# The last attention of a four-layer gated block on Trainium2: context tile of the weighting one unit later, rows of reciprocals by transposes, head 0's maximum in two parts

## The chip, the cores and the metric

The kernel runs on one core of one Trainium2 chip. It computes a chain of four gated cross-attention and feed-forward layers in one launch. The metric is the device time of one execution in microseconds, and the time of a kernel is the median over its runs. Engines are named as the profile names them: PE (matmuls and transposes; PEld is its weight load), DVE (vector work), ACT (activations and copies), POOL (copies), SP (it issues DMAs).

## The reference, cut to what matters

Eight sub-layers follow each other. The change is in the seventh, the last attention. Its queries come from the tokens of two batches (1024 tokens of 256 numbers each), its keys and values from the 1024 normalised token rows and the 77 normalised context rows of the same batch, with 16 heads of 64:

```python
def _L3_xattn_ref(x, latents, mask, g_x, b_x, g_l, b_l, Wq, Wkv, Wout, g_o, b_o):
    xn = layer_norm(x, g_x, b_x)
    ln = layer_norm(latents, g_l, b_l)
    q = jnp.einsum('bnd,de->bne', ln, Wq)
    kv_in = jnp.concatenate([xn, ln], axis=1)
    k, v = jnp.split(jnp.einsum('bnd,de->bne', kv_in, Wkv), 2, axis=-1)
    q, k, v = (split_heads(q), split_heads(k), split_heads(v))
    sim = jnp.einsum('bhid,bhjd->bhij', q * scale, k)
    attn = jax.nn.softmax(jnp.where(full_mask[:, None, None, :], sim, max_neg), axis=-1)
    out = jnp.einsum('bhij,bhjd->bhid', attn, v)
    return layer_norm(jnp.einsum('bne,ed->bnd', out.transpose(0, 2, 1, 3).reshape(b, m, INNER), Wout), g_o, b_o)

x = x + jnp.tanh(g_xattn[3]) * _L3_xattn_ref(ctx_1024, _layernorm(x), mask, ...)
```

In the call the block's tokens take the place of `latents` and the 77 context rows that of `x`. So each query has 1101 scores: 77 under the mask (context) and 1024 of tokens. All of it is fp32.

## The kernel before, in words

The stage works in 128 units. A unit is 128 queries of two neighbouring heads (h = 0 and 1) of one batch; eight units (u % 8 is the block of queries) make one pair of heads n = u // 8, and two units make one group g = u // 2. Each engine has its own program over the loop index u, and they meet by semaphores. PE works through this at each index u:

- `scores(u)`: four score blocks of 128 x 512 tokens and two of 128 x 77 context columns, into PSUM banks 0 to 4. Head 0 has words 0 to 1100 and head 1 words 1459 to 2559. They may start once both exponentials of unit u-1 have read their scores (semaphore `a6_p`).
- `ctx_turn(u-1)`: two transposes (L1214, L1215) of the context columns of the weights of unit u-1.
- At even u, `sums_turn`: the reciprocals of the sums of the group g = (u-2)/2 are spread over 64 partitions and turned into rows, by four matmuls with the identity matrix.
- At even u below 120, two of the eight pieces of the next pair's queries, keys and values (u % 8 = 0, 2, 4, 6 takes pieces 0 and 1, 2 and 3, 4 and 5, 6 and 7).
- At odd u, `weigh((u-3)/2)`: nine tiles of keys (eight of tokens, one of the context), two heads each, into one bank. This is 18 matmuls, and 36 in the trace, since an fp32 matmul stands there as two.
- At even u for the last four groups of each batch (`(u//2-2) % 32 >= 28`, so u = 60 to 66 and 124 to 130), `project`: the output projection, 16 matmuls of 256 columns, 32 in the trace.
- At eight odd u (N7), a transpose of rows for the next stage.

An fp32 matmul of a whole array is long: 256 columns take about 0.21 us for each of the two that the trace shows.

DVE: at even u it first multiplies the weighted values of a group by its rows of reciprocals (L2516). Then for every unit it adds the mask to the context scores (L2519), takes the maximum of head 1's context (L2520), that of head 0's 1101 scores (L2522), that of head 1's 1024 tokens (L2523), joins the two of head 1 (L2524), transposes the weights in 32 x 32 blocks once they are there (L2532, twice), and at odd u takes four reciprocals (L2537). ACT: copies the context transposes out of PSUM (L1781), at even u the rows of reciprocals (L1785), then takes the two exponentials with their sums (L1796), and at even u copies the two pieces (L1748 to L1756). POOL and SP's DMAs move the transposed blocks of the weights into place for `weigh` (16 blocks of a unit, half of them each).

The transposes, rows, pieces and products that leave PE share three PSUM banks (5, 6, 7) in turn: each takes the bank of the one three before it, once that one has been copied. The order is written out by hand in all five programs, and every engine works strictly in its own order.

## Time and profile before

| | |
|---|---|
| median of 3 runs | 2086.64 us (2085.38 to 2089.72) |
| the profiled execution | 2084.4 us |
| its span | 2082.6 us |
| PE busy | 1921.5 us, 92% |
| DVE busy | 1435.7 us, 69% |
| ACT busy | 978.5 us, 47% |
| POOL busy | 752.3 us, 36% |
| the stage of the change | from about 1105 us to about 1989 us of the span |

The profile shows one execution. The 128 units of the last attention take most of 885 us. A timeline row gives start, length, engine, line, operation, what is written and read, and how many instructions were merged into it; a bracket gives the idle time before it and what ended it. The sum of lengths of PE is more than the time, since a matmul's end is modelled and the next starts before it. A unit's length is best read from one first context transpose (L1214) to the next.

### The profile page before, as it was taken

The numbers are of one execution on the slowest core, as the hardware profiler recorded it, in microseconds if no ns is written. First come the engines' busy times: TensorE is split into PE (matmuls) and PEld (weight loads), VectorE is DVE, ScalarE is ACT, GpSimd is POOL, SyncE is SP. The second block draws the span as 40 slices with busy tenths as digits, with TensorE's granted clock in tenths as the row PEclk, the third lists the DMA queues.
The fourth block names the chain that finished last, engine by engine and source line by source line (L and its number), as shares of the span: only waits on it lengthen the run. The fifth ranks groups of instructions, "written<-read, shape, count | busy, mean of one in ns | idle before, by whom it ended". The sixth has DMA issues, their size and how long they took to land.

```text
span 2082.6 us, 33216 instructions
## 1 busy us (share of the span) xinstructions
PE 1921.5 (92%) x11797; PEld 1355.2 (65%) x11797; DVE 1435.7 (69%) x2676; ACT 978.5 (47%) x2079; POOL 752.3 (36%) x1145
## 2 busy tenths in 40 slices
PE   6997799696999988997878999999999999998999
PEld 3885799542699976883565666666675666655644
DVE  5775111467344457787867999999878999998755
ACT  5672333343111252226875555555545555555455
POOL 1002111000522200000006777777656777777500
PEclk9897899898999999998989999999999999999999
DMA  3702899502489960002002333333222333333201
GB/s 115 208 2 79 273 323 333 170 1 86 163 292 321 310 228 1 1 1 86 1 13 60 82 83 82 83 83 83 72 57 72 82 82 82 82 82 81 63 1 41
DMA packets 191184, 226.87 MB, mean 109 GB/s; under 512 B 28939, under 2 KB 167085, under 8 KB 191021
## 3 DMA queue, kind: packets, MB, share of 16 engines
q1 hardware_dynamic: 183725, 201.98, 33.0%
q0 software_dynamic: 7296, 22.78, 3.3%
q8 instruction: 95, 1.56, 0.3%
q14 instruction: 68, 0.56, 0.1%
HBM read 127.64 MB, written 29.91 MB: 76 GB/s over the span
## 4 chain that ended last, share of the span: by engine, by line
PE 45%; ACT 6%; DVE 3%; issue 1%; POOL 0%; ACTq 0%; DVEq 0%; POOLq 0%
PE ps L640 41%; ACT w_odd L1796 4%; PE ps L1214 2%; PE ps L1215 1%; ACT arena L1785 1%; PE ps L1106 0%; DVE w_odd L2532 0%; DVE small L2410 0%; POOL arena L1908 0%; ACT out_feat L1708 0%; PE ps L1115 0%; ACT xn_tok L1651 0%; DVE small L2522 0%; ACT out_feat L1714 0%; DVE arena L2380 0%
## 5 line engine op out<-in xcount | busy, mean ns | idle before, releaser
L1908 POOL COPY arena<-w_odd 32x512 f32<-32x512 f32 x1024 | 623.7, 609 | 254.4 <-DVE w_odd L2532 202.1
L640 PE MATMUL ps<-arena,w_odd 128*128 128x128 f32 (+4 forms) x2352 | 468.2, 441 | 3.0 <-DVE arena L2202 1.2
L640 PE MATMUL ps<-arena 128*64 128x256 f32 (+4 forms) x3248 | 392.3, 370 | 8.3 <-DVE arena L2333 4.4
L640 PEld LDWEIGHTS ps<-arena 128*64 128x64 f32 (+4 forms) x3248 | 258.9, 155 | 119.5 <-issue 22.6
L2532 DVE STREAM_TRANSPOSE w_odd<-w_odd 128x1024 f32<-128x1024 f32 x256 | 317.4, 1245 | 14.6 <-ACT w_odd L1796 3.0
L1796 ACT ACTIVATE w_odd<-ps,small 128x1101 f32<-128x1101 f32 x256 | 301.6, 1179 | 48.0 <-DVE small L2522 41.0
L640 PEld LDWEIGHTS ps<-arena,w_odd 128*128 128x128 f32 (+3 forms) x2352 | 286.3, 188 | 27.9 <-issue 18.7
L1781 ACT ACTIVATE arena<-ps 77x256 f32<-77x256 f32 x128 | 48.5, 379 | 295.4 <-PE ps L1215 295.4
L2522 DVE TENSOR_REDUCE small<-ps 128x1 f32<-128x1101 f32 x128 | 166.9, 1304 | 29.3 <-PE ps L640 28.1
L1893 POOL DMA_INDIRECT token_rows<-arena x62 | 59.8, 964 | 292.3 <-DVE arena L2223 292.3
L2523 DVE TENSOR_REDUCE small<-ps 128x1 f32<-128x1024 f32 x128 | 155.4, 1214 | 0.0
L640 PE MATMUL ps<-xn_feat,w_even 128*128 128x512 f32 (+1 forms) x352 | 139.5, 528 | 5.1 <-DVE xn_feat L2446 2.1
L1889 POOL DMA_INDIRECT expert_rows_in<-xn_tok,arena x48 | 46.4, 966 | 266.3 <-DVE arena L2186 252.3
L640 PEld LDWEIGHTS ps<-w_even,w_odd 64*128 64x128 f32 x512 | 86.5, 188 | 85.3 <-ACT w_odd L1796 65.9
L1903 POOL TENSOR_TENSOR x_res<-x_res,w_even 128x4096 f32<-128x4096 f32 x1 | 8.8, 8843 | 350.6 <-ACT xn_tok L1767 350.6
L640 PE MATMUL ps<-w_even,w_odd 64*128 64x77 f32 x512 | 100.8, 277 | 20.5 <-ACT w_odd L1796 19.9
L1580 ACT ACTIVATE arena<-ps,arena 128x128 f32<-128x128 f32 x184 | 67.3, 367 | 93.1 <-PE ps L640 82.3
L640 PE MATMUL ps<-arena,w_even 128*128 128x256 f32 (+2 forms) x608 | 107.6, 330 | 0.5 <-DVE x_res L1983 0.5
L640 PE MATMUL ps<-xn_feat,w_odd 128*128 128x512 f32 x224 | 103.5, 603 | 0.0
L640 PE MATMUL ps<-w_even,xn_feat 128*128 128x128 f32 (+1 forms) x576 | 100.9, 322 | 1.3 <-DVE xn_tok L2516 1.3
L640 PE MATMUL ps<-w_odd,arena 128*128 128x256 f32 (+1 forms) x436 | 101.5, 380 | 0.0
L640 PEld LDWEIGHTS ps<-arena,w_even 128*128 128x128 f32 x608 | 94.7, 192 | 8.4 <-DVE x_res L1983 0.6
(398 smaller groups left out, 2909.8 us busy)
## 6 DMA issues: line engine op xcount, KB each, us to landing
arena<-w_odd SPq DMA_DIRECT2D x1024, 64.0 KB
w_odd<-in_s_w SPq DMA_DIRECT2D x32, 1024.0 KB, 7.4
w_odd<-in_s_wgu SPq DMA_DIRECT2D x30, 704.0 KB, 6.1
w_even<-in_s_w SPq DMA_DIRECT2D x15, 1024.0 KB, 7.3
arena<-expert_rows_in SPq DMA_DIRECT2D x62, 130.0 KB, 4.7
w_odd<-in_s_wd SPq DMA_DIRECT2D x30, 256.0 KB, 3.6
out_feat<-in_s_wgu SPq DMA_DIRECT2D x10, 704.0 KB, 5.9
expert_rows_in<-zero_row POOLq DMA_DIRECT2D x1, 5070.0 KB, 33.2
```

What stands on the lines that cost most here:

```text
L640: return pe.matmul(o, lhsT, rhs, start=start, stop=stop, **kw)
L1214: pe.transpose(PS[0:C, bank, 0:P], s6_p[u % 2][0][:, S:KV], ident[:, :])
L1215: pe.transpose(PS[0:C, bank, P:2 * P], s6_p[u % 2][1][:, 0:C], ident[:, :]).then_inc(r6_mm, 1)
L1580: act.activation(s1_h[q][:, m], PS[:, (M * i + m) % 4, 0:TS], ACT.Gelu, bias=s1_bt[w][:, m:m + 1]).then_inc(per["mu_act", 1], 1)
L1781: act.activation(s6_ptc[g % 2][:, :, c0:c0 + P], PS[0:C, bank, 0:2 * P].rearrange("p (h n) -> p h n", h=2), ACT.Copy).then_inc(r6_act, 1)
L1796: act.activation(s6_p[u % 2][h], s6_sc[h], ACT.Exp, bias=s6_nm[:, u % 2, h:h + 1], accum_out=s6_sm[:, g % 2, 2 * (u % 2) + h:2 * (u % 2) + ...
L1889: pool.indirect_dma_start(xs_dram[st], bass.IndirectOffsetOnAxis(ap=pos_i[:, j, t:t + 1], axis=0), XNE[:, t, :], None)\
L1893: pool.indirect_dma_start(yt_dram[st], bass.IndirectOffsetOnAxis(ap=es_t[:, i:i + 1], axis=0), mx_y[st][i % 2][:, 0], None)\
L1908: pool.tensor_copy(s6_d[u % 4][32 * j:32 * j + 32, :, 256 * i:256 * i + 256], s6_pm[u % 2][32 * i:32 * i + 32, :, 256 * j:256 * j + 256]). ...
L2522: dve.tensor_reduce(s6_nm[:, u % 2, 0:1], s6_sc[0], AX.X, ALU.max, negate=True).then_inc(a6_mx, 1)
L2523: link(dve.tensor_reduce(s6_cm[:, u % 2, 1:2], psf[:, 3 * 512:3 * 512 + S], AX.X, ALU.max, negate=True))
L2532: dve.transpose(s6_pm[u % 2][:, h], s6_pm[u % 2][:, h]).then_inc(t6_done, 1)
```

## The change

Three things are changed in the last attention.

The context tile of `weigh` leaves the odd index. `weigh_tokens(g)` does the eight token tiles at u = 2g+3, and `weigh_context(g)` the ninth at u = 2g+4, behind `sums_turn`. Its products have bank 5 for themselves, while everything else alternates between banks 6 and 7. The multiplication by the reciprocals on DVE moves from the head of the even unit to its end, and the projection comes two indices later (`u//2-3` for `u//2-2`), so it stands at u = 62 to 68 and 126 to 132.

The rows of reciprocals are made by transposes. ACT copies the four reciprocals of a group into a 128 x 256 tile (`s6_rb`, each of them 64 times; L1800 of the change), with a new semaphore `r6_bc`; PE waits for it and transposes the two halves (L1227 of the change) in place of four matmuls.

Head 0's maximum is taken in two parts: words 0 to 511 (bank 0), which are full when the mask may be added, and words 512 to 1100 after the last scores. A third reduction of the two results gives the negated maximum.

PE, an odd unit and the even one behind it (u % 8 = 6), before. L640 is the helper of all matmuls; `ps<-arena 64x256` are the products of weights and values, `ps<-ident,small` the rows of reciprocals, `w_odd` holds queries and weights, `xn_feat` the normalised tokens.

```order
L640 MATMUL ps<-arena 64x256 x18
L640 MATMUL ps<-w_even,w_odd 128x77
L640 MATMUL ps<-arena,w_odd 128x512 x2
L640 MATMUL ps<-w_even,w_odd 128x77
L640 MATMUL ps<-arena,w_odd 128x512 x2
L1214 MATMUL ps<-ident,w_odd 77x128
L1215 MATMUL ps<-ident,w_odd 77x128
L640 MATMUL ps<-ident,small 64x128 x4
L640 MATMUL ps<-w_even,xn_feat 128x128 x8
L640 MATMUL ps<-xn_feat,w_even 128x256 x2
```

The same place in the change (L643 is the helper now, L1219 and L1220 the context transposes):

```order
L643 MATMUL ps<-arena 64x256 x16
L643 MATMUL ps<-w_even,w_odd 128x77
L643 MATMUL ps<-arena,w_odd 128x512 x2
L643 MATMUL ps<-w_even,w_odd 128x77
L643 MATMUL ps<-arena,w_odd 128x512 x2
L1219 MATMUL ps<-ident,w_odd 77x128
L1220 MATMUL ps<-ident,w_odd 77x128
L1227 MATMUL ps<-ident,arena 128x128 x2
L643 MATMUL ps<-arena 64x256 x2
L643 MATMUL ps<-w_even,xn_feat 128x128 x8
L643 MATMUL ps<-xn_feat,w_even 128x256 x2
```

Two of the 18 products have moved behind the rows of reciprocals of the even unit; and these are two transposes of `arena` (the new tile) where four matmuls of `small` stood.

ACT, an even unit (u % 8 = 2), before: context transposes, rows of reciprocals, two exponentials, three copies of pieces.

```order
L1781 ACTIVATE arena<-ps 77x2x128
L1785 ACTIVATE arena<-ps 128x256
L1796 ACTIVATE w_odd,small<-ps,small 128x1101 x2
L1752 ACTIVATE arena<-ps 128x256
L1756 ACTIVATE w_even<-ps 128x77
L1748 ACTIVATE w_odd<-ps 128x512
```

And in the change, where L1800 is the new copy of the reciprocals:

```order
L1794 ACTIVATE arena<-ps 77x2x128
L1800 ACTIVATE arena<-small 128x256
L1804 ACTIVATE arena<-ps 128x256
L1815 ACTIVATE w_odd,small<-ps,small 128x1101 x2
L1765 ACTIVATE arena<-ps 128x256
L1769 ACTIVATE w_even<-ps 128x77
L1761 ACTIVATE w_odd<-ps 128x512
```

The new copy stands between the copy of the context transposes (L1794) and that of the rows (L1804), ahead of the exponentials.

DVE, the end of an odd unit and the even unit behind it, before:

```order
L2532 STREAM_TRANSPOSE w_odd<-w_odd 128x1024 x2
L2537 RECIPROCAL small<-small 128x4
L2516 TENSOR_TENSOR out_feat<-ps,arena 128x256
L2519 TENSOR_TENSOR ps<-ps,w_even 128x2x77
L2520 TENSOR_REDUCE small<-ps 128x1
L2522 TENSOR_REDUCE small<-ps 128x1
L2523 TENSOR_REDUCE small<-ps 128x1
L2524 TENSOR_REDUCE small<-small 128x1
```

And in the change:

```order
L2546 STREAM_TRANSPOSE w_odd<-w_odd 128x1024 x2
L2551 RECIPROCAL small<-small 128x4
L2531 TENSOR_TENSOR ps<-ps,w_even 128x2x77
L2532 TENSOR_REDUCE small<-ps 128x1
L2533 TENSOR_REDUCE small<-ps 128x1
L2535 TENSOR_REDUCE small<-ps 128x1
L2536 TENSOR_REDUCE small<-small 128x1
L2537 TENSOR_REDUCE small<-ps 128x1
L2538 TENSOR_REDUCE small<-small 128x1
L2546 STREAM_TRANSPOSE w_odd<-w_odd 128x1024 x2
L2558 TENSOR_TENSOR out_feat<-ps,arena 128x256
```

The multiplication (L2516, now L2558) has gone from ahead of the mask (L2519, now L2531) to behind the two block transposes of the even unit; head 0's maximum is L2533, L2535 and L2536 in place of L2522.

```diff
@@ -220,6 +220,7 @@
         s6_k = [cut(AR, 9216 + 1024 * i, S) for i in range(2)]
         s6_v = [cut(AR, 11264 + 1152 * i, NKT, P) for i in range(2)]
         s6_r = [cut(AR, 13568 + 256 * i, 2 * P) for i in range(2)]
+        s6_rb = [cut(AR, 14080 + 256 * i, 4, DH) for i in range(2)]
         s6_z = [cut(AR, 14592 + 512 * i, 2, D) for i in range(2)]
         s6_cnt = cut(AR, 15616, KD, B * C)
         s6_mb = small[:, 568:568 + 40].bitcast(U8)[:, 0:B * C].rearrange("p (b c) -> p b c", b=B)
...
@@ -383,12 +385,12 @@
             batch = [("c", u - 1)] if turn else []
             if even and 2 <= u < NU + 2:
                 batch += [("r", (u - 2) // 2)]
+            if even and 4 <= u < NU + 4:
+                batch += [("v", (u - 4) // 2)]
             if even and u // 8 < 15:
                 batch += [("w", u // 8 + 1, u % 8), ("w", u // 8 + 1, u % 8 + 1)]
-            if not even and 3 <= u < NU + 3:
-                batch += [("v", (u - 3) // 2)]
-            if even and u >= 4 and (u // 2 - 2) % 32 >= 28:
-                batch += [("o", u // 2 - 2)]
+            if even and u >= 6 and (u // 2 - 3) % 32 >= 28:
+                batch += [("o", u // 2 - 3)]
             if u in N7:
                 batch += [("n", N7[u])]
             for key in batch:
...
@@ -396,13 +398,14 @@
                 done[eng] += 1
                 r6_no[key] = len(r6_no)
                 r6_sb[key] = (r6_act if eng == "act" else r6_dve, done[eng])
-        r6_keys = list(r6_no)
+        r6_keys = [key for key in r6_no if key[0] != "v"]
+        r6_turn = {key: i for i, key in enumerate(r6_keys)}
 
         PIECES = (("q", 0, 512), ("k", 768, S), ("v", 0, 2), ("q", 512, S), ("v", 6, NKT), ("k", 0, 512), ("v", 2, 6), ("k", 512, 768))
 
         def r6_bank(key):
 
-            return 5 + r6_no[key] % 3
+            return 5 if key[0] == "v" else 6 + r6_turn[key] % 2
 
         def copied(eng, key):
 
...
@@ -1175,9 +1178,11 @@
 
                 def free_bank(key):
 
-                    t = r6_no[key]
-                    if t >= 3:
-                        copied(pe, r6_keys[t - 3])
+                    if key[0] == "v":
+                        if key[1]:
+                            copied(pe, ("v", key[1] - 1))
+                    elif r6_turn[key] >= 2:
+                        copied(pe, r6_keys[r6_turn[key] - 2])
                     return r6_bank(key)
 
                 def scores(u):
...
@@ -1216,32 +1221,38 @@
 
                 def sums_turn(g):
 
-                    pe.wait_ge(a6_rb, g + 1)
+                    pe.wait_ge(r6_bc, g + 1)
                     bank = free_bank(("r", g))
                     for i in range(2):
-                        for h in range(2):
-                            r = 64 * h
-                            last = mm(PS[r:r + 64, bank, i * P:(i + 1) * P], s6_rc[:, g % 2, 2 * i + h:2 * i + h + 1].broadcast_to([P, DH]), ident[:, :])
+                        last = pe.transpose(PS[:, bank, i * P:(i + 1) * P], s6_rb[g % 2][:, 2 * i:2 * i + 2].rearrange("p a b -> p (a b)"), ident[:, :])
                     last.then_inc(r6_mm, 1)
 
-                def weigh(g):
+                def weigh_tile(g, i, bank):
 
                     n = g // 4
+                    s0 = 2 * g % 4
+                    rows = P if i < NKT - 1 else C
+                    for h in range(2):
+                        r = 64 * h
+                        if i < NKT - 1:
+                            p = s6_dw[:, s0:s0 + 2, h].rearrange("p u (q i n) -> p u q i n", q=4, i=8)[:, :, :, i]
+                        else:
+                            p = s6_ptc[g % 2][:, h]
+                        last = mm(PS[r:r + 64, bank, 0:2 * P], s6_v[n % 2][0:rows, i, r:r + 64], p, start=(i == 0), stop=(i == NKT - 1))
+                    return last
+
+                def weigh_tokens(g):
+
                     moved(pe, 2 * g)
                     moved(pe, 2 * g + 1)
+                    bank = free_bank(("v", g))
+                    for i in range(NKT - 1):
+                        weigh_tile(g, i, bank)
+
+                def weigh_context(g):
+
                     copied(pe, ("c", 2 * g + 1))
-                    bank = free_bank(("v", g))
-                    s0 = 2 * g % 4
-                    for i in range(NKT):
-                        rows = P if i < NKT - 1 else C
-                        for h in range(2):
-                            r = 64 * h
-                            if i < NKT - 1:
-                                p = s6_dw[:, s0:s0 + 2, h].rearrange("p u (q i n) -> p u q i n", q=4, i=8)[:, :, :, i]
-                            else:
-                                p = s6_ptc[g % 2][:, h]
-                            last = mm(PS[r:r + 64, bank, 0:2 * P], s6_v[n % 2][0:rows, i, r:r + 64], p, start=(i == 0), stop=(i == NKT - 1))
-                    last.then_inc(r6_mm, 1)
+                    weigh_tile(g, NKT - 1, r6_bank(("v", g))).then_inc(r6_mm, 1)
 
                 def project(g):
 
...
@@ -1273,13 +1284,15 @@
                         ctx_turn(u - 1)
                     if even and 2 <= u < NU + 2:
                         sums_turn((u - 2) // 2)
+                    if even and 4 <= u < NU + 4:
+                        weigh_context((u - 4) // 2)
                     if even and n < 16:
                         for i in (j, j + 1):
                             piece(n, i, free_bank(("w", n, i))).then_inc(r6_mm, 1)
                     if not even and 3 <= u < NU + 3:
-                        weigh((u - 3) // 2)
-                    if even and u >= 4 and (u // 2 - 2) % 32 >= 28:
-                        project(u // 2 - 2)
+                        weigh_tokens((u - 3) // 2)
+                    if even and u >= 6 and (u // 2 - 3) % 32 >= 28:
+                        project(u // 2 - 3)
                     if u in N7:
                         t = N7[u]
                         pe.wait_ge(ln_xn, NT * xn_no[ln_no[7]] + t + 1)
...
@@ -1781,6 +1794,12 @@
                         act.activation(s6_ptc[g % 2][:, :, c0:c0 + P], PS[0:C, bank, 0:2 * P].rearrange("p (h n) -> p h n", h=2), ACT.Copy).then_inc(r6_act, 1)
                     if even and 2 <= u < NU + 2:
                         g = (u - 2) // 2
+                        act.wait_ge(a6_rb, g + 1)
+                        if g >= 2:
+                            act.wait_ge(r6_mm, r6_no["r", g - 2] + 1)
+                        act.activation(s6_rb[g % 2], s6_rc[:, g % 2].unsqueeze(2).broadcast_to([P, 4, DH]), ACT.Copy).then_inc(r6_bc, 1)
+                    if even and 2 <= u < NU + 2:
+                        g = (u - 2) // 2
                         bank = filled(("r", g))
                         act.activation(s6_r[g % 2], PS[:, bank, 0:2 * P], ACT.Copy).then_inc(r6_act, 1)
                     if u < NU:
...
@@ -2507,19 +2526,14 @@
                     piece(0, j, j).then_inc(c6_sb, 1)
                 for u in range(NU + 6):
                     even = u % 2 == 0
-                    if even and 4 <= u < NU + 4:
-                        g = (u - 4) // 2
-                        c = (g // 4) % 8
-                        q0 = 2 * P * (g % 4)
-                        bank = filled(("v", g))
-                        copied(dve, ("r", g))
-                        dve.tensor_tensor(s6_ot[c][:, q0:q0 + 2 * P], PS[:, bank, 0:2 * P], s6_r[g % 2], ALU.mult).then_inc(r6_dve, 1)
                     if u < NU:
                         dve.wait_ge(a6_s, 4 * u + 3)
                         link(dve.tensor_tensor(s6_both, s6_both, s6_mk[:, u // 64].unsqueeze(1).broadcast_to([P, 2, C]), ALU.add))
                         dve.tensor_reduce(s6_cm[:, u % 2, 0:1], s6_both[:, 1], AX.X, ALU.max, negate=True)
+                        dve.tensor_reduce(s6_hm[:, u % 2, 0:1], psf[:, 0:512], AX.X, ALU.max, negate=True)
                         dve.wait_ge(a6_s, 4 * u + 4)
-                        dve.tensor_reduce(s6_nm[:, u % 2, 0:1], s6_sc[0], AX.X, ALU.max, negate=True).then_inc(a6_mx, 1)
+                        link(dve.tensor_reduce(s6_hm[:, u % 2, 1:2], psf[:, 512:KV], AX.X, ALU.max, negate=True))
+                        dve.tensor_reduce(s6_nm[:, u % 2, 0:1], s6_hm[:, u % 2], AX.X, ALU.min).then_inc(a6_mx, 1)
                         link(dve.tensor_reduce(s6_cm[:, u % 2, 1:2], psf[:, 3 * 512:3 * 512 + S], AX.X, ALU.max, negate=True))
                         dve.tensor_reduce(s6_nm[:, u % 2, 1:2], s6_cm[:, u % 2], AX.X, ALU.min).then_inc(a6_mx, 1)
                     if u == 0:
...
@@ -2533,14 +2547,21 @@
                         if not even:
                             g = u // 2
                             if g >= 2:
-                                dve.wait_ge(r6_mm, r6_no["r", g - 2] + 1)
+                                dve.wait_ge(r6_bc, g - 1)
                             dve.reciprocal(s6_rc[:, g % 2], s6_sm[:, g % 2]).then_inc(a6_rb, 1)
-                    if even and u >= 6 and 28 <= (u // 2 - 3) % 32 < 31:
-                        added(u // 2 - 3)
-                    if even and u >= 4 and (u // 2 - 2) % 32 >= 28:
-                        normed(u // 2 - 2)
-                    if not even and u >= 5 and ((u - 1) // 2 - 2) % 32 == 31:
-                        added((u - 1) // 2 - 2)
+                    if even and 4 <= u < NU + 4:
+                        g = (u - 4) // 2
+                        c = (g // 4) % 8
+                        q0 = 2 * P * (g % 4)
+                        bank = filled(("v", g))
+                        copied(dve, ("r", g))
+                        dve.tensor_tensor(s6_ot[c][:, q0:q0 + 2 * P], PS[:, bank, 0:2 * P], s6_r[g % 2], ALU.mult).then_inc(r6_dve, 1)
+                    if even and u >= 8 and 28 <= (u // 2 - 4) % 32 < 31:
+                        added(u // 2 - 4)
+                    if even and u >= 6 and (u // 2 - 3) % 32 >= 28:
+                        normed(u // 2 - 3)
+                    if not even and u >= 7 and ((u - 1) // 2 - 3) % 32 == 31:
+                        added((u - 1) // 2 - 3)
                     if u == 72:
                         row_vars7(0)
                     if u == 74:
```

## Rows read from the trace of the kernel before

**Rows 1.** Busy time by engine, one window (us, instructions); then clock, DMA share, GB/s
```profile
1200.00:1300.00 100.00, 98.97 (x680) 61.93 (x678) 90.88 (x125) 55.48 (x107) 75.43 (x125) 1.00 0.35 84
```

**Rows 2.** Timeline (start, length), PE: first context transpose, units 20 to 25
```profile
1230.68 0.33 PE L1214 MATMUL ps<-ident,w_odd 128*77 128x128 f32 x1
...
1237.02 0.34 PE L1214 MATMUL ps<-ident,w_odd 128*77 128x128 f32 x1
...
1243.58 0.34 PE L1214 MATMUL ps<-ident,w_odd 128*77 128x128 f32 x1
...
1249.82 0.33 PE L1214 MATMUL ps<-ident,w_odd 128*77 128x128 f32 x1
...
1256.37 0.33 PE L1214 MATMUL ps<-ident,w_odd 128*77 128x128 f32 x1
...
1262.61 0.34 PE L1214 MATMUL ps<-ident,w_odd 128*77 128x128 f32 x1
```

**Rows 3.** Timeline of units 24 and 25, all engines
```profile
1254.23 0.69 PE L640 MATMUL ps<-arena,w_odd 64*128 64x512 f32 x1
...
1255.06 0.13 DVE L2537 RECIPROCAL small<-small 128x4 f32<-128x4 f32 x1
...
1255.65 0.33 DVE L2519 TENSOR_TENSOR ps<-ps,w_even 128x154 f32<-128x154 f32 x1
...
1256.01 0.24 DVE L2520 TENSOR_REDUCE small<-ps 128x1 f32<-128x77 f32 x1
...
1256.48 1.30 DVE L2522 TENSOR_REDUCE small<-ps 128x1 f32<-128x1101 f32 x1 [0.23 <-PE ps L640]
...
1256.74 0.66 PE L640 MATMUL ps<-ident,small 128*64 128x128 f32 x8
...
1256.85 0.38 ACT L1781 ACTIVATE arena<-ps 77x256 f32<-77x256 f32 x1 [2.99 <-PE ps L1215]
...
1257.33 2.85 PE L640 MATMUL ps<-xn_feat,w_even 128*128 128x512 f32 x8
...
1257.44 0.38 ACT L1785 ACTIVATE arena<-ps 128x256 f32<-128x256 f32 x1 [0.22 <-PE ps L640]
...
1257.90 1.18 ACT L1796 ACTIVATE w_odd<-ps,small 128x1101 f32<-128x1101 f32 x1
...
1258.98 0.19 ACT L1796 ACTIVATION_READ_ACCUMULATOR w_odd<-ps,small 128x1 f32 x1
...
1260.47 0.33 PE L640 MATMUL ps<-w_even,w_odd 64*128 64x77 f32 x1 [0.29 <-ACT w_odd L1796]
...
1262.98 4.11 PE L640 MATMUL ps<-arena 128*64 128x256 f32 x36
...
1267.02 0.33 PE L640 MATMUL ps<-w_even,w_odd 64*128 64x77 f32 x1
```

**Rows 4.** Timeline, PE, unit 62: fourth pair of pieces, then the projection
```profile
1508.55 2.05 PE L640 MATMUL ps<-w_even,xn_feat 128*128 128x128 f32 x16
...
1511.30 1.89 PE L640 MATMUL ps<-w_even,xn_tok 128*128 128x256 f32 x8
```

**Rows 5.** Groups by line and shape: an ACT copy from SBUF, two DVE maxima
```profile
L1640 ACT ACTIVATE arena<-arena 128x256 f32<-128x256 f32 x16 | 6.4, 401 | 0.0
...
L2522 DVE TENSOR_REDUCE small<-ps 128x1 f32<-128x1101 f32 x128 | 166.9, 1304 | 29.3 <-PE ps L640 28.1
...
L2520 DVE TENSOR_REDUCE small<-ps 128x1 f32<-128x77 f32 x128 | 30.4, 237 | 4.4
```

**Rows 6.** Timeline, PE, the last projections (units 128 to 130)
```profile
1970.42 2.00 PE L640 MATMUL ps<-w_even,xn_tok 128*128 128x256 f32 x8
...
1977.53 4.11 PE L640 MATMUL ps<-arena 128*64 128x256 f32 x36
...
1982.16 2.00 PE L640 MATMUL ps<-w_even,xn_tok 128*128 128x256 f32 x8 [0.53 <-DVE out_feat L2516]
```

**Rows 7.** Busy time by engine in a window without pieces (units 122 and 123)
```profile
1923.00:1930.00 7.00, 3.93 (x21) 2.45 (x20) 5.34 (x7) 3.27 (x6) 4.74 (x9) 0.79 0.30 72
```

7 lines of the change are left out of this document (4 added, 3 removed).

## The prediction

> **What bounds the kernel now.** I read the busy time by window first: in the middle of the stage PE is at 98.97 of 100 us, DVE at 90.88, ACT at 55.48, with a granted clock of 1.00 [rows 1]. That alone says nothing of what ends last, so I took one cycle of units from the first context transposes of the timeline [rows 2]. Odd units last 6.55 us (from 1249.82 to 1256.37). Even units last 6.34 us at u = 20 and 6.24 us at u = 22 and 24; u % 8 = 2 goes like u = 20. So there are two limits.
>
> The timeline of u = 24 shows the first one [rows 3]. Call S the start of its scores, 1254.23. The scores are ready at S+2.25, where DVE begins head 0's maximum (1256.48); this takes 1.30; the first exponential starts at S+3.67 (1257.90); two exponentials, 2.57 us, lead to the next scores at 1260.47, S+6.24. This chain of scores, maximum, two exponentials and scores is the limit of even units at u % 8 = 0 and 6. The second limit is PE's own work. In the odd unit the products start at 1262.98 and the next scores at 1267.02: 4.04 us for 36 matmuls, 0.112 each, and they end 0.31 us after the chain would have allowed. At u % 8 = 2 and 4 the pieces are longer and PE is over by 0.10.
>
> In the even unit PE reaches the rows of reciprocals at 1256.74 (S+2.51), and the pieces at 1257.33 (S+3.10) [rows 3].
>
> **The change, odd units.** Four matmuls of the trace go: 4 x 0.112 = 0.45. PE would be at 6.10, so the chain is the limit. Its part that changes is the maximum. Two rows give its cost: 77 elements take 0.237 and 1101 take 1.304 [rows 5], so 1.042 ns an element and a fixed 0.157. The mask is added at S+1.42 and head 1's context maximum starts at S+1.78 [rows 3]. Head 0's first part can follow about 0.16 later, at S+1.94, and the second at S+2.54 (a start-to-start of about 0.60, with 0.08 of overlap); by then all scores are there. It takes 0.157 + 589 x 0.001042 = 0.77 and ends at S+3.31; the small joining reduction is another 0.16 with 0.03 before it, S+3.50. Before it was S+3.55 (1256.48 + 1.30). So the split gives 0.05, not the half maximum that one might expect: its first part hides under the scores, but the second has its own fixed cost and so has the third. I take 6.20 for an odd unit, 0.35 less. Bounds: 0.25 less (the parts cost 0.1 more than I think) and 0.40 less. There are 60 such units (u = 3 to 125 without two that are longer for other reasons), so -21.0 us, with -15 and -24 as bounds.
>
> The Trainium skill speaks against the split: "VectorE: DVE Perf Modes", section on the errata of operands in SBUF, says that an operation pays its fixed latency once for a large tile and again for each small one. Its figures, 120 cycles at 0.96 GHz for a PSUM source and 58 for SBUF, give an estimate of 0.19 us for the two added reductions. The rows give 0.16 for each, 0.24 with the overlap of 0.08 taken off. By the page an odd unit would come out 0.05 shorter, 3 us in the sum; the measured durations stand.
>
> **The change, even units.** Here is the new wait. PE may not transpose the reciprocals until ACT has spread them, and ACT does that behind the copy of the context transposes, which PE has made just before. The reciprocals themselves are there early (1255.06, S+0.83) [rows 3] and ACT is idle for 2.99 us before the copy (bracket of 1256.85) [rows 3], but the new copy stands behind that one in ACT's order. So: context copy at S+2.62; 0.38 long with 0.10 of overlap with what follows (1257.90 + 1.18 against 1258.98) [rows 3], so the spreading starts at S+2.90; an ACT copy of 128 x 256 from SBUF takes 0.40 [rows 5]; PE goes on at S+3.35, with 0.05 for the semaphore (as 0.04 to 0.05 from a last exponential to the scores). PE idles 0.84 us where it idled none. Two transposes cost 0.30 (the two context transposes took 0.37, 1256.37 to 1256.74 [rows 2, 3], and matmul rows of 128 columns as short as 0.11 each), in place of 0.59. Then the context tile, 4 x 0.112 = 0.45. The pieces start at S+4.10 for S+3.10: 1.00 later. Queued behind the wait on PE are the context tile, both pieces and the next scores. Bounds: 0.76 later (spreading 0.35, transposes 0.22, context 0.43) and 1.15 later (no overlap on ACT, transposes 0.37).
>
> ACT's exponentials are late too. The rows leave PE about 0.48 after the first transpose starts (1256.37 to 1256.85, the same for the context) [rows 2, 3], S+3.83; the copy of the rows holds ACT for 0.28; the first exponential starts at S+4.11 in place of S+3.67. The chain is 6.24 + 0.43 = 6.67, with +0.28 and +0.59 as bounds. The maximum is ready long before, so the split gives nothing here.
>
> Which of both limits counts depends on the pieces:
> - u % 8 = 0: pieces 2.57 (2.85 busy, less some 0.28 by which the last modelled end passes the next start) [rows 3]. PE 6.67, chain 6.67: +0.43. 13 units without a projection: +5.6.
> - u % 8 = 2 and 4: PE was the limit, so all of it counts: 28 units x 1.00 = +28.0.
> - u % 8 = 6: pieces 2.75 (1508.55 to 1511.30) [rows 4]; 4.10 + 2.75 = 6.85 for 6.24: 14 x 0.61 = +8.5.
> - 4 units with pieces and projection, PE bound: 4 x 1.00 = +4.0.
> - u = 120, 122, 124 without pieces +0.43 each, 126 with a projection +1.00: +2.3.
>
> Sum +48.4; with the bounds +35 and +57. The other edits here cost nothing: the multiplication on DVE ends at about S+8.2 (two block transposes of 2.5 us in all from S+5.4, then 0.3), when the mask of the next unit is due at S+6.67+1.42 = S+8.09 or later, so 0.1 at most at u % 8 = 0; PE's banks are free in time, as each one's copy is over a unit before.
>
> **The end of the stage.** A projection takes 7.1 us (1970.42 to 1977.53) [rows 6]. At u = 124 none is left, so that unit falls from 10.0 (3.10 + 6.9) to 6.67, -3.4. At the end there is one more than before: u = 128 holds an earlier group's, and behind the last weighting (from 1977.53, 4.04 long) stand two instead of one: +7.0. The wait before the last (1977.53 + 4.04 to 1982.16, some 0.6, of which DVE's multiplication) goes: -0.6; the spreading behind the reciprocals at u = 128 adds 0.3 there. Net +3.3. The first batch's projections move into like units, +0.
>
> Sum: 48.4 - 21.0 + 3.3 = +30.7 us. Against the profiled execution's 2084.4 that is 2115.1. The median of the runs is 2086.64, 2.2 above that execution, so 2117 for the median. With all bounds on one side: 35 - 24 + 3 = +14 (2101) and 57 - 15 + 4 = +46 (2133).
>
> **The rivals.**
> 1. The spreading is hidden. If ACT had spread the reciprocals before S+2.5, PE would not wait: pieces at S+2.51+0.30+0.45 = S+3.26, only 0.16 later. Then u % 8 = 2 and 4 and projections cost 32 x 0.16 = 5.1, the rest nothing, odd units -21.0, the end +3.3: -12.6, 2074. For it: the reciprocals are ready at S+0.83 and ACT idles. Against it: ACT's order in the change. It decides the sign: the change is faster if the spreading ends before about S+2.9 instead of S+3.3. Chance 0.06.
> 2. The stall is partly covered and the gain and the loss cancel, 2083 to 2091: it needs a shift of the pieces of about 0.4, outside my bounds. Chance 0.05.
> 3. The split makes the chain longer. If the maximum begins only when the last scores are there (a first part that waits, or a late DVE), the three take 0.60 + 0.77 + 0.03 + 0.16 = 1.56 in place of 1.30, and the chain of the 60 odd units is 6.50 instead of 6.20: +18, so 2135. For it DVE is at 91% [rows 1]; against it is the idle of 0.23 before head 0's maximum in the same unit [rows 3]. Chance 0.12.
> 4. PE's clock. In a stretch where PE was busy 3.93 of 7.00 us the granted clock was 0.79 [rows 7], so in part the lower level of 1.2 GHz; in the middle of the stage it was 1.00 [rows 1]. The change puts 0.84 us of idle into every even unit. If a tenth of the units had their scores (2.2 us long) at 1.2 GHz, 2.2 us each more, that is 13 x 2.2 = +29: 2146. Against it: with 0.84 idle in 13.2 us PE is still busy over 90%, while rows 7 have 56%. Chance 0.08. The Trainium skill, "TensorE: Matmul & The Clock Gate", part on the transpose in PE mode, says that transposes do not count as busy for the clock; two more of them would then make this rival likelier, but the context transposes stand in every unit of rows 1 at a clock of 1.00, so I give it no more.
>
> **How the numbers follow.** My forecast has 0.69, rivals 1 to 4 have 0.06, 0.05, 0.12 and 0.08. A change of under 0.2% (4 us) can't be told from none. Faster is rival 1 and a bit of 2: 0.07; within 0.2%: 0.05; slower the rest: 0.88. Range 2100 to 2136: the forecast's bounds and rival 3, leaving out rivals 1, 2 and 4.
>
> **What would show it.** In the profile after: the copy by ACT of `arena` from `small` starts about 0.28 after the context copy, and PE's transposes of `arena` have some 0.8 us of idle before them, released by ACT; odd units are 6.2 and even ones 6.7, 7.3, 7.3 and 6.85 long; the second part of head 0's maximum ends about 3.3 after the scores' start. It is wrong if PE has no idle before those transposes, if odd units stay at 6.5, or if the clock of the middle falls below 1.00.

## The result, and the profile after

The changed kernel takes 2139.07 us (median of 4 runs, 2135.69 to 2140.45); the kernel before took 2086.01 beside it (4 runs). The ratio is 1.0249 [1.0231, 1.0267]. The direction was forecast; the forecast of 2117 is 22 us too low, and the time lies above the range. The profiled execution took 2140.45 us with a span of 2138.7, 56.1 more than before.

The busy time of the same window as [rows 1], after:

```profile
1200.00:1300.00 100.00, 94.00 (x594) 56.51 (x596) 87.24 (x147) 54.57 (x111) 71.91 (x119) 1.00 0.33 79
```

PE has lost 5 us of 100 to idle, at an unchanged clock of 1.00. The first context transposes, which answer to [rows 2], for u = 19 to 23:

```profile
1233.46 0.33 PE L1219 MATMUL ps<-ident,w_odd 128*77 128x128 f32 x1
1239.63 0.33 PE L1219 MATMUL ps<-ident,w_odd 128*77 128x128 f32 x1
1247.18 0.33 PE L1219 MATMUL ps<-ident,w_odd 128*77 128x128 f32 x1
1253.34 0.33 PE L1219 MATMUL ps<-ident,w_odd 128*77 128x128 f32 x1
1260.50 0.33 PE L1219 MATMUL ps<-ident,w_odd 128*77 128x128 f32 x1
```

Odd units last 6.17 and 6.16 (6.55 before), the even one at u = 20 (u % 8 = 4) lasts 7.55 (6.34) and that at u = 22 (u % 8 = 6) 7.16 (6.24). The timeline of unit 22, all engines, answers to [rows 3]; its scores start at S = 1251.20:

```profile
1251.20 0.33 PE L643 MATMUL ps<-w_even,w_odd 64*128 64x77 f32 x1
...
1252.35 0.14 DVE L2551 RECIPROCAL small<-small 128x4 f32<-128x4 f32 x1
1252.63 0.33 DVE L2531 TENSOR_TENSOR ps<-ps,w_even 128x154 f32<-128x154 f32 x1
...
1253.14 0.68 DVE L2533 TENSOR_REDUCE small<-ps 128x1 f32<-128x512 f32 x1
...
1253.74 0.76 DVE L2535 TENSOR_REDUCE small<-ps 128x1 f32<-128x589 f32 x1
1253.82 0.38 ACT L1794 ACTIVATE arena<-ps 77x256 f32<-77x256 f32 x1 [2.67 <-PE ps L1220]
1254.10 0.40 ACT L1800 ACTIVATE arena<-small 128x256 f32<-128x256 f32 x1
1254.54 0.15 DVE L2536 TENSOR_REDUCE small<-small 128x1 f32<-128x2 f32 x1
1254.56 0.44 PE L1227 MATMUL ps<-ident,arena 128*128 128x128 f32 x2 [0.77 <-ACT arena L1800]
...
1254.93 0.65 PE L643 MATMUL ps<-arena 77*64 77x256 f32 x4
1255.03 0.38 ACT L1804 ACTIVATE arena<-ps 128x256 f32<-128x256 f32 x1 [0.53 <-PE ps L1227]
1255.32 1.18 ACT L1815 ACTIVATE w_odd<-ps,small 128x1101 f32<-128x1101 f32 x1
1255.51 2.05 PE L643 MATMUL ps<-w_even,xn_feat 128*128 128x128 f32 x16
...
1258.36 0.33 PE L643 MATMUL ps<-w_even,w_odd 64*128 64x77 f32 x1
```

PE has finished both context transposes and stands for 0.77 us until ACT has spread the reciprocals (L1800), which it does at once behind the context copy (L1794). The reciprocals had been there since 1252.49, and ACT idle for 2.67 before the copy. From the first context transpose to the transposes of the spread tile it is 1.22, where the old rows followed after 0.37: 0.85 more. The same wait stands in every even unit. All instructions of L1227 on PE:

```profile
L1227 PE MATMUL ps<-ident,arena x128: 272/327/475, 1119.7 to 2016.3; 128*128 128x128 f32 x128
its engine sat idle before it (us, times) until:
  ACT arena L1800: 50.1, 64
```

50.1 us in 64 waits. In step with it the exponential starts at S+4.12 (forecast S+4.11), and the pieces at S+4.31 where they stood at S+3.10. The split of the maximum ends at S+3.49 (1254.54 + 0.15; forecast S+3.50).

Where the 56.1 us of span went, by the first context transposes (c0 is that of index 1, c119 that of index 120; the last line goes from c125, at index 126, to the end of the program):

| stretch | before | after | difference | forecast |
|---|---|---|---|---|
| ahead of c0 | 1107.07 | 1110.62 | +3.55 | 0 |
| c0 to c119 | 801.13 | 842.83 | +41.7 | +26.1 |
| c119 to c125 | 45.61 | 44.32 | -1.3 | -3.1 |
| behind c125 | 128.8 | 140.9 | +12.1 | +7.7 |

The first line is not the change's: the instructions there are the same, and four experiments below that leave them as they are too have c0 at 1107.29, 1107.46, 1109.67 and 1110.15. The granted clock of 600 to 800 was 0.95 in this execution and 0.98 before. The last line is the end of the stage, PE, which answers to [rows 6]:

```profile
2016.01 0.69 PE L1227 MATMUL ps<-ident,arena 128*128 128x128 f32 x2 [1.34 <-ACT arena L1800]
2016.62 1.12 PE L643 MATMUL ps<-arena 77*64 77x256 f32 x4
2017.68 3.78 PE L643 MATMUL ps<-w_even,xn_tok 128*128 128x256 f32 x8
2021.25 2.67 PE L643 MATMUL ps<-w_even,out_feat 128*128 128x256 f32 x8
2023.76 1.89 PE L643 MATMUL ps<-w_even,xn_tok 128*128 128x256 f32 x8
...
2027.30 4.11 PE L643 MATMUL ps<-arena 128*64 128x256 f32 x36
2031.34 1.99 PE L643 MATMUL ps<-w_even,xn_tok 128*128 128x256 f32 x8
```

and the busy time and clock of two windows there:

```profile
2010.00:2020.00 10.00, 7.67 (x44) 4.55 (x41) 7.47 (x14) 6.55 (x11) 4.14 (x7) 0.80 0.12 28
2020.00:2030.00 10.00, 10.00 (x54) 7.78 (x54) 2.79 (x11) 0.45 (x2) 0.88 (x2) 0.86 0.11 26
```

Two projections do stand behind the last weighting, as forecast. What was not forecast: PE was idle for 0.99 and 1.34 us a little earlier, and from 2016 to 2022 the granted clock is 0.50, the lower level of 1.2 GHz. The first half of the projection takes 6.08 (2017.68 to 2023.76), the second 3.54 (to 2027.30).

### The profile page after: what moved, and what is told of

The parts are those of the page before. It is cut to its first block, busy times and chain, and to the rows that moved or that the text cites. A ratio compares the mean times of both kernels' runs of the same rounds, so it can differ in the third digit from the quotient of the medians.

```text
span 2138.7 us, 32768 instructions
## 1 busy us (share of the span) xinstructions
PE 1933.3 (90%) x11413; PEld 1341.3 (63%) x11413; DVE 1447.9 (68%) x2932; ACT 994.8 (47%) x2143; POOL 752.6 (35%) x1145
## 4 chain that ended last, share of the span: by engine, by line
PE 46%; ACT 5%; DVE 3%; issue 2%; POOL 0%; ACTq 0%; DVEq 0%
PE ps L643 41%; ACT w_odd L1815 2%; PE ps L1219 1%; PE ps L1227 1%; ACT arena L1800 1%; PE ps L1220 1%; PE ps L1109 1%; DVE w_odd L2546 0%; DVE small L2429 0%; ACT L1826 0%; PE ps L1118 0%; ACT xn_tok L1664 0%; ACT out_feat L1721 0%; DVE small L2535 0%; DVE arena L2502 0%
## 5 line engine op out<-in xcount | busy, mean ns | idle before, releaser
L643 PE MATMUL ps<-arena,w_odd 128*128 128x128 f32 (+4 forms) x2352 | 470.6, 443 | 3.0 <-DVE arena L2221 1.2
L643 PE MATMUL ps<-arena 128*64 128x256 f32 (+4 forms) x3248 | 406.8, 373 | 8.2 <-DVE arena L2352 4.4
L2546 DVE STREAM_TRANSPOSE w_odd<-w_odd 128x1024 f32<-128x1024 f32 x256 | 312.9, 1243 | 46.4 <-ACT w_odd L1815 40.1
L643 PEld LDWEIGHTS ps<-arena 128*64 128x64 f32 (+4 forms) x3248 | 252.9, 155 | 121.9 <-issue 33.8
L643 PEld LDWEIGHTS ps<-arena,w_odd 128*128 128x128 f32 (+3 forms) x2352 | 287.0, 189 | 27.6 <-issue 18.8
L1794 ACT ACTIVATE arena<-ps 77x256 f32<-77x256 f32 x128 | 48.6, 379 | 294.5 <-PE ps L1220 294.5
L643 PE MATMUL ps<-xn_feat,w_even 128*128 128x512 f32 (+1 forms) x352 | 139.5, 528 | 4.9 <-DVE xn_feat L2465 2.1
L643 PEld LDWEIGHTS ps<-w_even,w_odd 64*128 64x128 f32 x512 | 86.9, 189 | 85.1 <-issue 42.3
L643 PE MATMUL ps<-w_even,w_odd 64*128 64x77 f32 x512 | 101.0, 278 | 18.3 <-ACT w_odd L1815 17.0
L643 PE MATMUL ps<-arena,w_even 128*128 128x256 f32 (+2 forms) x608 | 107.8, 330 | 0.5 <-DVE x_res L2002 0.5
L643 PE MATMUL ps<-xn_feat,w_odd 128*128 128x512 f32 x224 | 103.7, 604 | 0.0
L643 PE MATMUL ps<-w_odd,arena 128*128 128x256 f32 (+1 forms) x436 | 101.5, 379 | 0.0
L643 PE MATMUL ps<-w_even,xn_feat 128*128 128x128 f32 (+1 forms) x576 | 100.8, 321 | 0.0
L643 PEld LDWEIGHTS ps<-arena,w_even 128*128 128x128 f32 x608 | 94.8, 192 | 8.6 <-DVE x_res L2002 0.6
L2535 DVE TENSOR_REDUCE small<-ps 128x1 f32<-128x589 f32 x128 | 97.2, 759 | 1.5 <-PE ps L643 1.5
```

Of the source, the lines that this page charges most:

```text
L643: return pe.matmul(o, lhsT, rhs, start=start, stop=stop, **kw)
L1794: act.activation(s6_ptc[g % 2][:, :, c0:c0 + P], PS[0:C, bank, 0:2 * P].rearrange("p (h n) -> p h n", h=2), ACT.Copy).then_inc(r6_act, 1)
L2535: link(dve.tensor_reduce(s6_hm[:, u % 2, 1:2], psf[:, 512:KV], AX.X, ALU.max, negate=True))
L2546: dve.transpose(s6_pm[u % 2][:, h], s6_pm[u % 2][:, h]).then_inc(t6_done, 1)
```

## The experiments

Ratios are to the kernel before, run beside each kernel. The experiments ran on more than one chip (before took 2087.03 beside the first four told here, 2099.88 and 2098.68 beside the others), so ratios are compared, not times.

**The spreading ahead of the context copy.** The changed kernel with one block of ACT moved.

```diff
+act.wait_ge(a6_rb, g + 1)
...
+act.activation(s6_rb[g % 2], s6_rc[:, g % 2].unsqueeze(2).broadcast_to([P, 4, DH]), ACT.Copy).then_inc(r6_bc, 1)
...
 bank = filled(("c", v))
...
-act.wait_ge(a6_rb, g + 1)
...
-act.activation(s6_rb[g % 2], s6_rc[:, g % 2].unsqueeze(2).broadcast_to([P, 4, DH]), ACT.Copy).then_inc(r6_bc, 1)
```

> The changed kernel with one edit: ACT spreads the reciprocals ahead of the copy of the context transposes instead of behind it. Theory 1 (the new wait of PE for ACT is what costs): the 0.77 us of idle before the transposes of the rows goes in all 64 even units; even units fall from 7.55 to 6.70 (u % 8 = 2, 4), from 7.09 to 6.25 (0) and from 7.16 to 6.33 (6); odd ones stay at 6.16 to 6.25; in all about 51 us less, 2088. Rival (the copies on ACT are the limit whatever their order, so the rows and the exponentials stay late): even units stay over 6.9 and the time over 2115.

Measured: 2083.3 us (8 runs), ratio 0.9977 [0.9966, 0.9988]. The timeline of an even unit (u % 8 = 6), ACT and PE:

```profile
1242.36 0.41 ACT L1795 ACTIVATE arena<-small 128x256 f32<-128x256 f32 x1 [1.37 <-DVE small L2551]
1243.18 0.33 PE L1219 MATMUL ps<-ident,w_odd 128*77 128x128 f32 x1
...
1243.46 0.38 PE L1227 MATMUL ps<-ident,arena 128*128 128x128 f32 x2
1243.66 0.38 ACT L1800 ACTIVATE arena<-ps 77x256 f32<-77x256 f32 x1 [0.89 <-PE ps L1220]
1243.78 0.65 PE L643 MATMUL ps<-arena 77*64 77x256 f32 x4
...
1244.36 2.05 PE L643 MATMUL ps<-w_even,xn_feat 128*128 128x128 f32 x16
1244.65 1.18 ACT L1815 ACTIVATE w_odd<-ps,small 128x1101 f32<-128x1101 f32 x1 [0.33 <-DVE small L2536]
```

The bracket of ACT's copy shows it: ACT waits for the reciprocal and for nothing else, and is done at 1242.77, 0.69 us before PE starts its transposes of the spread tile (1243.46). In 63 of 64 even units no idle of PE stands before those transposes, and the exponential waits for the maximum again. Even units are 6.57 or 6.56 (u % 8 = 2, 4), 6.17 (6) and 6.14 (0) long, most odd ones away from the projections 6.16 to 6.28. So the wait made the change slow: 1.0249 to 0.9977 is some 56 us (3.3 of them are a lower clock at the end of the stage, told further down). The two context transposes took 0.28 here (1243.18 to 1243.46), where I had kept 0.37 in the expectation; that is most of why the even units came out 0.11 to 0.16 shorter than expected, and the time 5 us. What is left of the change is faster than before, by 4.8 us (2.5 to 7.1 by the interval) and not by the 12.6 of rival 1; the runs below say why.

**The split alone** (in the kernel before).

```diff
+dve.tensor_reduce(s6_hm[:, u % 2, 0:1], psf[:, 0:512], AX.X, ALU.max, negate=True)
 dve.wait_ge(a6_s, 4 * u + 4)
-dve.tensor_reduce(s6_nm[:, u % 2, 0:1], s6_sc[0], AX.X, ALU.max, negate=True).then_inc(a6_mx, 1)
+link(dve.tensor_reduce(s6_hm[:, u % 2, 1:2], psf[:, 512:KV], AX.X, ALU.max, negate=True))
+dve.tensor_reduce(s6_nm[:, u % 2, 0:1], s6_hm[:, u % 2], AX.X, ALU.min).then_inc(a6_mx, 1)
```

> The kernel before with head 0's maximum in two parts and nothing else. Theory 1 (the first part hides under the scores, the fixed costs eat the rest): the units at the limit of the chain (u % 8 = 0 and 6) fall from 6.24 to 6.19, the others stay; 2084 to 2087. Rival (the two extra reductions lengthen the chain): even units 6.4 to 6.5 and the time 2092 to 2100.

Measured: 2086.64 (10 runs), 0.9998 [0.9988, 1.0008]. The units that the chain bounds (u % 8 = 0, 6) fall from 6.24 to 6.16 or 6.17; the other even units and most odd ones stay at PE's bound. The four odd units behind a projection of the first batch (u = 61 to 67) grow by 0.23 to 0.26, to 6.78, 6.94, 6.85 and 6.85: about 1 us, which takes back half of what the 27 others gave. Nothing in the sum, and rival 3 shows in those four units alone.

**The context tile alone**, with its bank and the later projections, rows by matmuls and one maximum (of the changed kernel).

```diff
-pe.wait_ge(r6_bc, g + 1)
+pe.wait_ge(a6_rb, g + 1)
...
-        last = pe.transpose(PS[:, bank, i * P:(i + 1) * P], s6_rb[g % 2][:, 2 * i:2 * i + 2].rearrange("p a b -> p (a b)"), ident[:, :])
+            last = mm(PS[r:r + 64, bank, i * P:(i + 1) * P], s6_rc[:, g % 2, 2 * i + h:2 * i + h + 1].broadcast_to([P, DH]), ident[:, :])
```

> The changed kernel with the rows of reciprocals by four matmuls as before (no spreading on ACT) and head 0's maximum in one piece; only the context tile, bank 5, the multiplication and the projection are moved. Theory 1 (a change between matmuls of half the array's columns and of the whole array costs PE about 0.1, and behind the four matmuls of the rows there is none for the context tile): the tile costs 0.45, pieces start 3.56 after the scores, even units 6.80 at u % 8 = 2 and 4, odd units 6.2; 2097 with 12 us more behind the last unit. Rival (the tile itself costs 0.58, for its 77 rows or its place): pieces at 3.69, 6.93, and 2103.

Measured: 2093.92 (6 runs), 1.0037 [1.0024, 1.0049], 3 us under the 2097 of theory 1, with its unit lengths. Even units 6.78 (2, 4), 6.38 (6) and 6.31 (0), odd ones 6.24 or 6.33. PE in an even unit:

```profile
1232.27 0.66 PE L643 MATMUL ps<-ident,small 128*64 128x128 f32 x8
1232.76 0.60 PE L643 MATMUL ps<-arena 77*64 77x256 f32 x4
1233.29 1.16 PE L643 MATMUL ps<-w_even,xn_feat 128*128 128x128 f32 x8
```

The rows take 0.49 here, start to start, and 0.59 in [rows 3], with the same eight matmuls. What differs is what follows: matmuls on half the columns of the array (`77*64`) here, on the whole array (`128*128`) there. So matmuls ahead of a change of shape cost PE about 0.10 us more, and most of that (0.08) stands in these 0.53 of the context tile too, where four times 0.112 would be 0.45. The early spreading has a third pair, within one kernel: two context transposes took 0.28 ahead of the whole array (1243.18 to 1243.46) and 0.37 ahead of products on half the columns (1237.02 to 1237.39).

**The transposes alone** (in the kernel before, ACT's spreading behind the context copy).

```diff
-pe.wait_ge(a6_rb, g + 1)
+pe.wait_ge(r6_bc, g + 1)
...
-            last = mm(PS[r:r + 64, bank, i * P:(i + 1) * P], s6_rc[:, g % 2, 2 * i + h:2 * i + h + 1].broadcast_to([P, DH]), ident[:, :])
+        last = pe.transpose(PS[:, bank, i * P:(i + 1) * P], s6_rb[g % 2][:, 2 * i:2 * i + 2].rearrange("p a b -> p (a b)"), ident[:, :])
...
+act.activation(s6_rb[g % 2], s6_rc[:, g % 2].unsqueeze(2).broadcast_to([P, 4, DH]), ACT.Copy).then_inc(r6_bc, 1)
```

> The kernel before with the rows of reciprocals by transposes alone, spread by ACT behind the context copy; weighting, projection, banks and maximum as before. Theory 1 (the wait): PE goes on with the rows 0.85 later and they take 0.37 for 0.59, so pieces start 0.63 later; even units 6.97 at u % 8 = 2 and 4 and 6.67 (the chain) at 0 and 6; odd units stay at 6.55; 2119. Rival (the loss comes from the moved context tile): 2090 or less.

Measured: 2109.82 (4 runs), 1.0106 [1.0089, 1.0123]. Even units 6.78 (2, 4) and 6.59 (0, 6), odd ones still 6.55.

```profile
1237.77 0.40 ACT L1787 ACTIVATE arena<-small 128x256 f32<-128x256 f32 x1
1238.23 0.44 PE L1224 MATMUL ps<-ident,arena 128*128 128x128 f32 x2 [0.77 <-ACT arena L1787]
1238.50 1.06 PE L642 MATMUL ps<-w_even,xn_feat 128*128 128x128 f32 x8
...
1251.83 1.95 PE L642 MATMUL ps<-w_even,xn_feat 128*128 128x128 f32 x16
...
1253.62 1.03 PE L642 MATMUL ps<-xn_feat,w_even 128*128 128x256 f32 x4
```

The wait of 0.77 is there without the other two edits, so it belongs to this one. The time came out 9 us below what I expected, mostly because the transposes take 0.27 where the whole array follows, and 0.37 where the column halves of the context tile do: the same 0.10 from the other side. Another 0.09 is gone behind them. The sixteen matmuls of pieces 6 take 1.79 here (1251.83 to 1253.62), behind transposes on the whole array; in the kernel before, behind the rows on half the columns, they took 1.88, from 1508.55 [rows 4] to:

```profile
1510.43 1.03 PE L640 MATMUL ps<-xn_feat,w_even 128*128 128x256 f32 x4
```

So a change of shape costs about 0.10 ahead of it and up to 0.09 behind it. The edit as a whole costs 23 us and not 56, because it also saves. At u % 8 = 2 and 4 the transposes of the spread tile start 1.22 behind the first context transpose for 0.37 (+0.85), take 0.27 for 0.59 (-0.32), and the pieces behind them 0.09 less: +0.44, as measured (6.78 for 6.35). Against the kernel with the early spreading, the change starts them 1.22 behind for 0.28, so there the wait is worth 0.94, and units grow by 0.99 (7.56 for 6.57).

**DVE writes the reciprocals spread** (of the changed kernel; ACT's copy goes).

```diff
-dve.reciprocal(s6_rc[:, g % 2], s6_sm[:, g % 2]).then_inc(a6_rb, 1)
+dve.reciprocal(s6_rb[g % 2], s6_sm[:, g % 2].unsqueeze(2).broadcast_to([P, 4, DH])).then_inc(a6_rb, 1)
```

> The changed kernel, but the spread reciprocals come from DVE: its reciprocal writes each of the four 64 times (256 elements for 4), and ACT has no spreading and PE no wait for ACT. Theory 1 (only the place of the spreading costs): like the spreading ahead of the context copy, 2083, even units 6.56 at u % 8 = 2 and 4 and 6.15 at 0 and 6. Rival (DVE is now the limit: the reciprocal is some 0.3 longer, and the mask of the even unit had 0.1 to 0.2 of room): even units 0.1 to 0.2 longer, 2086 to 2092.

Measured: 2169.69 (4 runs), 1.0326 [1.031, 1.0342]. A miss for all theories. The group of the line:

```profile
L2545 DVE RECIPROCAL arena<-small 128x256 f32<-128x256 f32 x64 | 109.4, 1710 | 0.0
```

1.71 us for 256 elements, where the changed kernel's reciprocals of 4 took 0.135: with the 1.04 ns an element of a maximum I had reckoned some 0.4. DVE is late with the mask and the maximum, PE waits 0.33 for the reciprocal ahead of its transposes, and even units grow to 7.49 (7.40 at u % 8 = 0).

**More spreading** (the changed kernel with a further ACT copy of 128 x 128 ahead of the spreading).

```diff
+act.activation(cut(AR, 16256, 4, 32), s6_rc[:, g % 2].unsqueeze(2).broadcast_to([P, 4, 32]), ACT.Copy)
 act.activation(s6_rb[g % 2], s6_rc[:, g % 2].unsqueeze(2).broadcast_to([P, 4, DH]), ACT.Copy).then_inc(r6_bc, 1)
```

> The changed kernel with a second, half as wide copy of the reciprocals on ACT (128 x 128, to a place that nothing reads) ahead of the spreading, so that the wait of PE is some 0.2 us longer. Theory 1 (PE waits for ACT there, and what is queued behind it is late by the same): the idle before the transposes of the rows grows from 0.77 by 0.20 and each of the 59 even units with pieces by as much; 12 us more than the changed kernel (ratio to before 1.031). Rival (the even unit is bound by something beside the wait): under 4 us more, 1.025 to 1.027.

Measured: 2163.99 (4 runs), 1.0308 [1.0291, 1.0325]. ACT and PE in an even unit:

```profile
1240.03 0.30 ACT L1800 ACTIVATE arena<-small 128x128 f32<-128x128 f32 x1
1240.23 0.40 ACT L1801 ACTIVATE arena<-small 128x256 f32<-128x256 f32 x1
1240.68 0.44 PE L1227 MATMUL ps<-ident,arena 128*128 128x128 f32 x2 [0.97 <-ACT arena L1801]
```

The copy adds 0.20 to ACT, 0.20 to PE's idle (0.97 for 0.77) and 0.20 to every even unit (7.76, 7.75, 7.35, 7.28 by median for u % 8 = 2, 4, 6, 0, where the change had 7.56, 7.55, 7.16, 7.09): 1.0308 - 1.0249 is 12 us. The path from ACT to the end has no slack in any even unit, those at u % 8 = 0 included.

**The projections later** (the kernel before, two indices later on all engines).

```diff
-if even and u >= 4 and (u // 2 - 2) % 32 >= 28:
-    project(u // 2 - 2)
+if even and u >= 6 and (u // 2 - 3) % 32 >= 28:
+    project(u // 2 - 3)
```

> The kernel before with the projection two indices later and nothing else. Theory 1 (each projection is 6.9 us of PE, and one of those of the last batch leaves the scores' region for the place behind the last weighting, where nothing hides it): the part from the 126th context transpose on grows by 7 us (128.8 to 136), the six units before it shrink by 3.5, the first batch's region stays within 1 us; 2089 to 2092. Rival (it is hidden anyway, since PE waits there for the moved weights): 2087 or less.

Measured: 2105.37 (8 runs), 1.0027 [1.0017, 1.0037], so +5.7 us. It is all at the end: behind c125 it is 135.0 for 128.8, as expected; between c119 and c125 it is 1.0 less, where I had expected 3.5; c58 to c71, the first batch's projections, are the same to 0.1. In c119 to c125 the granted clock was 0.85 here and 0.93 in the kernel before; how much of the missing 2.5 us that took was not separated.

**The banks alone** (the kernel before with the products in bank 5, all else in 6 and 7).

```diff
-return 5 + r6_no[key] % 3
+return 5 if key[0] == "v" else 6 + r6_turn[key] % 2
```

> The kernel before with only the banks of the change: the weighted values in bank 5, everything else in turn in banks 6 and 7. Theory 1 (two banks in turn cost only where a projection follows pieces): the four units with both grow by 0.5 to 1 us, 3 us in all, the others stay at 6.24, 6.35 and 6.55; ratio 1.001 to 1.002. Rival (the alternation also holds back pieces or context transposes in every unit): 1.005 or more.

Measured: 2102.28 (10 runs), 1.0016 [1.0004, 1.0027]. Units without a projection are as before to 0.01. Those with one in the first batch are 13.83, 13.89, 13.88 and 13.81 long for 13.25, 12.85, 12.79 and 13.26: 3.3 us together, as expected. In unit 62 the projection, which followed the pieces at once in [rows 4], waits:

```profile
1506.80 1.96 PE L641 MATMUL ps<-w_even,xn_tok 128*128 128x256 f32 x8 [0.35 <-ACT arena L1757]
```

With two banks in turn it needs the copy of a piece, and ACT takes that behind both exponentials. I had counted this part of the change at nothing ("PE's banks are free in time").

**As before at the projections** (the first experiment's kernel; the last four groups of each batch are weighed and projected at the old places).

```diff
+def late(g): return g % 32 < 28
...
-if even and 4 <= u < NU + 4:
+if even and 4 <= u < NU + 4 and late((u - 4) // 2):
     weigh_context((u - 4) // 2)
```

> The changed kernel with the spreading ahead of the context copy, and for the last four groups of each batch (those with a projection) the weighting, the multiplication and the projection as in the kernel before. Theory 1 (the three costs of the change are the wait, the end and the two regions of projections): 2072, with units as in the run with the spreading first (6.16 odd; 6.56 and 6.16 even), and 129 us from the 126th context transpose on. Rival (the region of projections is bound by DVE whatever the order): 2078 to 2083.

Measured: 2091.33 (6 runs), 0.9953 [0.994, 0.9965]. Better than the first one by 0.24%, half of what was expected: behind c125 it is 130.8, 2.0 above the kernel before, but projecting units stay at 13.76 to 13.90, by the wait for banks that the experiment above shows.

**The same without the split.**

```diff
-dve.tensor_reduce(s6_hm[:, u % 2, 0:1], psf[:, 0:512], AX.X, ALU.max, negate=True)
 dve.wait_ge(a6_s, 4 * u + 4)
-link(dve.tensor_reduce(s6_hm[:, u % 2, 1:2], psf[:, 512:KV], AX.X, ALU.max, negate=True))
-dve.tensor_reduce(s6_nm[:, u % 2, 0:1], s6_hm[:, u % 2], AX.X, ALU.min).then_inc(a6_mx, 1)
+dve.tensor_reduce(s6_nm[:, u % 2, 0:1], s6_sc[0], AX.X, ALU.max, negate=True).then_inc(a6_mx, 1)
```

> The kernel of the run before this one, with head 0's maximum in one piece. Theory 1 (the split takes 0.07 off the chain of each unit whose limit is the chain, now all odd ones and the even ones at u % 8 = 0 and 6, some 85): 2078, odd units 6.24. Rival (the split is worth nothing or costs): 2070 to 2073.

Measured: 2095.88 (12 runs), 0.998 [0.997, 0.999]. The split is worth 0.27% here, as theory 1 had it, and nothing in the kernel before: it pays once the odd units have come down to the chain.

**The projections in bank 5 too.**

```diff
-return 5 if key[0] == "v" else 6 + r6_turn[key] % 2
+return 5 if key[0] in "vo" else 6 + r6_turn[key] % 2
```

> The version with the spreading first and the last four groups of each batch as before, with the projections in bank 5 (the bank of the weighted values, read by then) instead of in turn with the pieces. Theory 1 (with two banks in turn a projection waits for the copy of a piece, which ACT makes only behind the exponentials): the idle of 0.3 to 1 us before the projections goes, units with pieces and a projection fall from 13.8 to 13.9 to 13.3 (u % 8 = 2, 4) and 12.9 (0, 6), 3 us in all; ratio 0.994 against 0.9953. Rival (no wait for the bank): no difference.

Measured: 2087.5 (6 runs), 0.995 [0.9934, 0.9965]. The four projecting units are back at 13.20, 12.81, 12.74 and 13.21, 3.3 us less in the four, as the theory of the banks had it; the time (0.995 against 0.9953) does not resolve it. By its ratio this is the best version and beats both kernels: 11 us below the one before, where the change as made is 53 above.

## Why the prediction was wrong in its size

**Odd units, -0.35 each: right.** They lost 0.38 (6.17 for 6.55), and 0.29 at u % 8 = 7, except the four behind a projection (below, rival 3). The split came out at S+3.49 for S+3.50. The Trainium skill's rule ("VectorE: DVE Perf Modes", section on the errata) is borne out in kind: a reduction of only 2 elements takes 0.155, the whole fixed part of 0.157 again. The same section adds that a fixed term of about 150 cycles was measured where its table has 58; at 0.96 GHz that is an estimate of 0.156, and the trace agrees with it and not with the 0.06 that 58 cycles give. My sum had gone by 0.16 from the rows.

**PE waits 0.84 for the spreading: right.** The transposes start 0.85 later than the rows did (1.22 for 0.37), released by ACT's copy, in 64 of 64 even units; moving the copy took the wait away, and 0.20 more of copying made it 0.20 longer. Rival 1 was wrong about the order and right that the sign hung on ACT's place. Its size was too large, 12.6 for the 4.8 measured: with the copy in front, the end still grew by 7.8 where the sum had 3.3, and the banks cost the 3.3 that it did not have. Rival 2 needed the pieces 0.4 later; they were 1.20 later.

**"The pieces start at S+4.10 for S+3.10: 1.00 later": the step that failed, by its size.** They start at S+4.31, 1.20 later. The wait was right; the transposes were 0.37 for 0.30 and the context tile 0.58 for 0.45. I had multiplied counts by the 0.112 of matmuls amid their like, and PE pays about 0.10 more where the shape on the array changes; here it changes twice, ahead of the context tile and behind it. 28 units at some 0.2 (7.56 for a forecast 7.35) make up to 5.9 us.

**Pieces of 2.57 and 2.75: too short as well.** At u % 8 = 0 they take 2.78 up to the next scores, and at 6 2.85 (1255.51 to 1258.36). For the first I had taken 0.28 off for the modelled end, and it is 0.07; for the second I had read a row where a projection follows on the whole array ([rows 4]), and scores follow on half the rows. So these units, forecast at 6.67 and 6.85, are PE's at 7.09 and 7.16, and grew by 0.85 and 0.92 for 0.43 and 0.61: 13 x 0.42 + 14 x 0.31 = 9.8 us. Counted unit by unit, both kinds together make 13.2 of the 15.6 that the table's second line is off (41.7 for 26.1); 5.9 and 9.8 are a little more, as some units (u = 2 and 74) grew by less than their like. The rest is 1.3 in the projecting units (+5.3 for +4.0) and 1.0 in the odd ones.

**Four projecting units +1.00 each: near, and partly by luck.** 57.4 for 52.2 us is +1.3 each. The banks alone cost 0.8 each in their experiment, which I had at 0 because each bank's copy was to be over a unit before: a second step that failed, hidden by an overlap with the wait that was not taken apart.

**The end, +3.3: too small.** One more projection behind the last weighting was right: +6.2 in the experiment that only moved it, +7.8 behind c125 (136.6) with the early spreading. The change has 4.3 more than that. About 1 is the wait in the last even unit; 3.3 are PE at 1.2 GHz, 2.5 in the projection (6.08 for 3.54) and 0.7 ahead of it (2016.01 to 2017.68 where 0.95 is usual, 1254.56 to 1255.51). So rival 4 was right at a place that I had not looked at, and wrong in the middle, where the clock stayed 1.00. What brought the clock down there is open: PE idled 0.99 and 1.34 us ahead of it, and with the early spreading it idled 0.91 and 1.34 at the same place and the granted clock was 1.00.

**c119 to c125, -3.1: too good.** It was -1.3. The granted clock of that stretch was 0.85 for the 0.93 before, and it was 0.85 as well in the experiment that only moved the projections; what the clock took of the missing 1.8 is open.

**Ahead of the stage, 3.55 us: not the change's**, and not to be forecast.

**The sum of the upper bounds** for even units comes to 58 and not 57, which changes nothing here.

**Rival 3** (a split that lengthens the chain) would have given 2135, near the time measured, by a mechanism that is not there in the common odd unit: that one is 6.17 or 6.26 long, and the split alone costs nothing in the sum. It is there in the four behind a projection of the first batch. At u = 63, DVE comes late from the normalisation of projected rows, with the scores all there (the next context transpose stands at 1559.40):

```profile
1559.88 0.68 DVE L2533 TENSOR_REDUCE small<-ps 128x1 f32<-128x512 f32 x1
1560.48 0.76 DVE L2535 TENSOR_REDUCE small<-ps 128x1 f32<-128x589 f32 x1
...
1561.28 0.16 DVE L2536 TENSOR_REDUCE small<-small 128x1 f32<-128x2 f32 x1
```

From 1559.88 to 1561.44 it is 1.56 in place of 1.30, the rival's own number. These units are 6.84 to 6.87 long in the change and with the early spreading, and 6.59 to 6.62 with one maximum (the context tile alone). That is 1 us in all. A time that fits is no evidence for its story; the unit lengths are.

## What to carry to other kernels

Before adding a producer to an engine that stands in program order, ask not whether it is idle but what stands ahead of the new instruction: ACT was idle for 2.7 us and the reciprocals were ready, and still a copy behind a late one cost some 50 us, while the same copy one place earlier left no wait on PE in 63 of 64 units. Price short runs of matmuls by a row with the same neighbours, since a change of shape added 0.1 us ahead of it and up to 0.1 behind, and check both limits of a unit when one shifts: two kinds of units went from the chain to PE. A buffer scheme with fewer buffers in turn must be priced where the work is densest (here the projecting units), not in the common unit.

## What the runs showed of the hardware

- A DVE reciprocal took 1.71 us for 128 x 256 and 0.135 for 128 x 4, so 6.25 ns an element against 1.04 of a maximum. The Trainium skill ("VectorE: DVE Perf Modes", section on the pipeline's hardware budget) says that the reciprocal is an iterative division that repeats; the row is in keeping with it, at 6 times a maximum's time.
- PE lost about 0.10 us ahead of a change between the whole array and half its columns: 0.37 against 0.27 for the same two transposes, 0.59 against 0.49 for the same eight matmuls, 0.37 against 0.28 for the same two context transposes. Behind such a change the first sixteen matmuls took 1.88 against 1.79.
- The granted clock was 0.50 from 2016 to 2022 in the change, behind idles of PE of 0.99 and 1.34 us, and 1.00 in the kernel with the early spreading, behind idles of 0.91 and 1.34 at the same place. What tells the two apart is open.
